# Five edits to the schedule of an attention-and-feed-forward kernel: lepe in four pieces, the reciprocal of the softmax sums on VectorE, the layer norm tiles spread, the first scores by single unit, the first rotations on VectorE alone

## The reference, cut to what matters

```python
qkv = x @ w_qkv.T + b_qkv                       # q, k, v in 16 heads of 16
q, k = elu(q) + 1, elu(k) + 1
q, k = rope(q), rope(k)                         # x1*cos - x2*sin, x1*sin + x2*cos
attn = softmax(q @ k.T / 4) @ v
lepe = depthwise conv of v along the rows, 3 taps, + b_lepe
x = layernorm(x + attn + lepe)                  # first layer norm
h = s0 * ([x, -x] @ K0); h = 2 * relu(h)        # K are matrices of +1 and -1
h = s1 * (h @ K1);       h = 2 * relu(h)
x = layernorm(x + s2 * (h @ K2))                # second layer norm
```

## Time and profile before

| | |
|---|---|
| median of 3 runs | 2399.99 us (2399.28 to 2402.57) |
| the profiled execution | 2403.18 us |
| its span, first to last instruction | 2401.3 us |
| PE busy | 2161.6 us (90%) |
| DVE busy | 1524.1 us (63%) |
| ACT busy | 1428.8 us (59%) |
| POOL busy | 1144.7 us (48%) |
| DVE reduce L908 | 1024 of 1213 ns |
| ACT exp L762 | 2048 of 607 ns |
| POOL reciprocal L1239 | 63 of 2909 ns |
| POOL lepe L1257 | 24 of 4524 ns |
| DMA, issue to landing: stacks, `k_scratch` (POOL), out, base | 2.0, 5.8, 4.1, 5.9 us |

### The profile page before, as it was taken

How to read it: one execution, slowest core, us unless ns; L and a number is a source line. 1 busy time by engine, 2 the same in 40 slices (tenths; PEclk the granted TensorE clock), 3 DMA queues, 4 the chain that set the end, 5 groups by cost and what they waited for, 6 DMA issues and landing times.

```text
span 2401.3 us, 41722 instructions
## 1 busy us (share of the span) xinstructions
PE 2161.6 (90%) x16960; PEld 839.9 (35%) x16960; DVE 1524.1 (63%) x1629; ACT 1428.8 (59%) x2601; POOL 1144.7 (48%) x726
## 2 busy tenths in 40 slices
PE   4397798999999999999989999999999999899977
PEld 2021222452225422354224622354223542244234
DVE  6766598329972499527983299725994279844432
ACT  1066597428883398625974198733986269833921
POOL 4519527662457527473276625475284733700200
PEclk8588899999999999999999999999999999899988
DMA  5001101001100101001110011001110011000000
GB/s 166 24 8 32 54 22 39 15 12 54 56 21 18 40 23 55 14 18 48 48 30 16 19 45 56 21 18 43 37 38 14 18 52 58 16 8 1 19 1 18
DMA packets 40272, 77.81 MB, mean 32 GB/s; under 512 B 15008, under 2 KB 19472, under 8 KB 36880
## 3 DMA queue, kind: packets, MB, share of 16 engines
q1 hardware_dynamic: 34896, 52.07, 7.6%
q0 software_dynamic: 5184, 23.07, 2.7%
HBM read 47.32 MB, written 25.17 MB: 30 GB/s over the span
## 4 chain that ended last, share of the span: by engine, by line
PE 55%; DVE 14%; POOL 14%; ACT 10%; issue 4%; DMA 3%; SPq 0%; ACTq 0%; POOLq 0%; DVEq 0%
PE unit_banks L670 23%; DVE maxima L908 11%; PE o_bank L592 9%; PE unit_banks L524 8%; ACT probs L762 8%; PE unit_banks L681 5%; PE unit_banks L629 4%; POOL work L1257 2%; POOL rden L1239 2%; PE unit_banks L641 2%; POOL base L1259 2%; DMA base<-in_x 1%; POOL base L1254 1%; POOL hres L1267 1%; PE unit_banks L534 1%
## 5 line engine op out<-in xcount | busy, mean ns | idle before, releaser
L908 DVE TENSOR_REDUCE maxima<-unit_banks 128x1 f32<-128x1024 f32 x1024 | 1190.3, 1213 | 134.3 <-PE unit_banks L524 129.6
L762 ACT ACTIVATE probs<-unit_banks 128x512 f32<-128x512 f32 x2048 | 1090.1, 607 | 298.7 <-PE unit_banks L534 286.5
L524 PE MATMUL unit_banks<-k_stack,q_stack 48*128 48x512 f16 x2048 | 637.0, 401 | 105.1 <-DVE maxima L908 63.4
L534 PE MATMUL unit_banks<-q_stack,k_stack 50*128 50x512 f16 x2048 | 666.2, 397 | 34.5 <-ACT probs L762 28.4
L592 PE MATMUL o_bank<-probs,v_pair 128*32 128x256 f32 x8192 | 667.3, 405 | 0.4 <-ACT probs L762 0.4
L670 PE MATMUL unit_banks<-h0T,w 128*128 128x512 f16 x2048 | 444.7, 379 | 0.0
L960 DVE SCALAR_TENSOR_TENSOR h1T<-unit_banks,h1T 128x1024 f16<-128x1024 f32 x64 | 78.4, 1224 | 414.8 <-ACT h1T L836 414.8
L1227 POOL TENSOR_TENSOR max_scaled<-maxima,ln_consts 128x16 f32<-128x16 f32 x63 | 14.6, 232 | 637.1 <-DVE maxima L908 619.9
L592 PEld LDWEIGHTS o_bank<-probs,v_pair 128*32 128x32 f32 x8192 | 171.6, 110 | 387.6 <-ACT probs L762 235.2
L524 PEld LDWEIGHTS unit_banks<-k_stack,q_stack 48*128 48x128 f16 x2048 | 117.5, 95 | 525.2 <-DVE maxima L908 279.3
L836 ACT ACTIVATE h1T<-unit_banks 128x1024 f16<-128x1024 f32 x64 | 65.5, 1023 | 388.3 <-PE unit_banks L670 388.3
(11 more groups left out here) (127 smaller groups left out, 1572.3 us busy)
## 6 DMA issues: line engine op xcount, KB each, us to landing
xT_sb<-in_xT SPq DMA_DIRECT2D x9, 1024.0 KB, 16.0
base<-in_x POOLq DMA_DIRECT2D x8, 1024.0 KB, 5.9
q_stack<-q_scratch SPq DMA_DIRECT2D x128, 64.0 KB, 2.0
k_stack<-k_scratch SPq DMA_DIRECT2D x128, 64.0 KB, 2.0
out<-hres SPq DMA_DIRECT2D x8, 1024.0 KB, 4.1
q_scratch<-parts POOLq DMA_DIRECT2D x14, 512.0 KB, 3.3
k_scratch<-parts POOLq DMA_DIRECT2D x14, 512.0 KB, 5.8
q_stack<-q_scratch SPq DMA_DIRECT2D x128, 32.0 KB, 1.9
```

Source lines behind the costliest of these rows:

```text
L524: return nc.tensor.matmul(units.half(unit[0], unit[1], half), q_stack[row:row + STACK, r, t * P:(t + 1) * P], k_stack[row:row + STACK, r, ...
L534: nc.tensor.matmul(units.half(kind, unit, 0), k_stack[row:end, r, kt * P:(kt + 1) * P], q_stack[row:end, r, half * 512:(half + 1) * 512], ...
L762: nc.scalar.activation(probs[:, 2 * (kt % 2) + h, half * 512:(half + 1) * 512], units.half(kind, unit, 0), ACT.Exp, scale=exp_regs[2 * j + ...
L908: nc.vector.reduce_max(maxima[:, parity, h * T + t:h * T + t + 1], units.both(kind, unit), AXIS_XY)\
```

## The change

Five parts. (1) `lepe` is dealt as two, two, two and one instructions behind pairs -1 to 2, and has its own temporary `lepe_tmp`, so ScalarE no longer waits for it before the projections; `ln_scales` stand right behind a piece of lepe (first layer norm) and behind `split_max` 4 (second); in batch 0 elu, rotation and split are dealt over pairs 0 to 5 with a `split_max` between every two. (2) `reciprocal_o` on VectorE in step 3 takes the place of the power on POOL. (3) `STATS_STEPS` and `NORMALISE_STEPS` are other tables. (4) In the start TensorE waits for one S unit at a time and finishes it. (5) Both first rotations are on VectorE, the high parts of the first split on ScalarE, and POOL begins lepe of batch 0 only when the first maxima are split. With these, SP loads the stack freed by pair j - 1 behind the max rows of pair j.

```diff
-STATS_STEPS = ((9, 10, 11, 12, 13, 14, 15, 16), (None, None, None, None, 35, 36, 37, 38))
-NORMALISE_STEPS = (2 * T + 6, 6 * T + 1)
+STATS_STEPS = ((7, 8, 9, 10, 11, 12, 13, 14), (None, None, None, None, 32, 33, 34, 35))
+NORMALISE_STEPS = ((17, 20, 21, 23, 25, 28, 29, 31), (37, 38, 39, 41, 44, 46, 47, 49))
...
+            def load_freed_stack(kind, b, j):
+                if j < 0:
+                    if kind != "first":
+                        units.wait_full(sp, "first" if b == 1 else "mid", b - 1, ("T", PAIRS - 1, T - 1, 0, 1))
+                        load_stacks(b, j + RING)
+                    return
+                if kind == "last" and j + RING >= PAIRS:
+                    return
+                units.wait_full(sp, kind, b, ("T", j, T - 1, 0, 1))
+                if j + RING < PAIRS:
+                    load_stacks(b, j + RING)
+                else:
+                    sp.wait_ge(scratch_written, b * 64 + 64)
+                    load_stacks(b + 1, j + RING - PAIRS)
...
-                    units.wait_full(sp, kind, b, ("T", j, T - 1, 0, 1))
-                    if j + RING < PAIRS:
-                        load_stacks(b, j + RING)
-                    else:
-                        sp.wait_ge(scratch_written, b * 64 + 64)
-                        load_stacks(b + 1, j + RING - PAIRS)
+                    load_freed_stack(kind, b, j - 1)
...
             def start_scores(v):
-                pair = [("S", -1, v, h) for h in range(2)]
                 for h in range(2):
-                    units.wait_free(pe, "start", 0, pair[h])
-                for half in range(2):
-                    for h in range(2):
-                        last = score_half(("start", pair[h]), v // T, v % T, h, half)
-                        if half == 1:
-                            last.then_inc(units.full_sem(pair[h]), 1)
+                    unit = ("S", -1, v, h)
+                    units.wait_free(pe, "start", 0, unit)
+                    for half in range(2):
+                        last = score_half(("start", unit), v // T, v % T, h, half)
+                    last.then_inc(units.full_sem(unit), 1)
...
+            for which, w in enumerate((work[:], work_of("start", 1))):
+                act.wait_ge(scale_made, SCALE_OPS[which])
+                for c, (src, dst) in enumerate(((w[:, 3], parts[:]), (w[:, 1], parts_b))):
+                    act.wait_ge(start_split, 8 * which + 3 + 3 * c)
+                    if which == 1:
+                        act.wait_ge(start_written[c], 16)
+                    nc.scalar.activation(dst[:, 0], src, ACT.Copy, scale=in_scale[:, which:which + 1]).then_inc(start_hi, 1)
...
+            def reciprocal_o(kind, b, j):
+                n = b * PAIRS + j
+                units.wait_read(dve, kind, b, ("O rows", j))
+                wait(dve, attn_written, n)
+                o = o_rows_sb[:, n % 2].rearrange("p (g c) -> p g c", c=32)
+                nc.vector.reciprocal(rden[:], o[:, :, D]).then_inc(reciprocal_done, 1)
...
+                            if h == 0 and kt == 3 and o_rows_pair(kind, j, 2) is not None:
+                                reciprocal_o(kind, b, j - 1)
...
-            rotate(combine, work_k, rotated)
+            pool.wait_ge(max_split, MAX_OPS)
...
-                    lepe(b, 0, 3)
+                    lepe(b, 0, 2)
                 split_max(kind, b, 1)
                 normalise_o(kind, b, 0)
                 if kind == "first":
                     elu(kind, b, 0)
-                    rotate_side(kind, 0)
                 else:
-                    lepe(b, 3, 6)
+                    lepe(b, 2, 4)
+                    ln_scales(b * 2 - 2, 0)
                 split_max(kind, b, 2)
                 normalise_o(kind, b, 1)
                 if kind == "first":
-                    split(kind, b + 1, 0)
-                    elu(kind, b, 1)
+                    rotate_side(kind, 0)
                 else:
-                    lepe(b, 6, 7)
-                    ln_scales(b * 2 - 2, 0)
+                    lepe(b, 4, 6)
                 split_max(kind, b, 3)
                 normalise_o(kind, b, 2)
                 if kind == "first":
-                    rotate_side(kind, 1)
-                    split(kind, b + 1, 1)
+                    split(kind, b + 1, 0)
+                else:
+                    lepe(b, 6, 7)
                 normalise_o(kind, b, 3)
+                if kind == "first":
+                    elu(kind, b, 1)
...
                 split_max(kind, b, 4)
+                if kind == "first":
+                    rotate_side(kind, 1)
+                else:
+                    ln_scales(b * 2 - 2, 1)
                 split_max(kind, b, 5)
                 normalise_o(kind, b, 4)
-                if kind != "first":
-                    ln_scales(b * 2 - 2, 1)
+                if kind == "first":
+                    split(kind, b + 1, 1)
```

61 lines of the change are left out of this document (21 added, 40 removed).

## The result

The changed kernel takes **2328.18 us** (median of 4 runs, 2321.91 to 2334.75), the kernel before 2400.51 in the same runs; the ratio is 0.9698, with a 95% interval of 0.9668 to 0.9728. It is faster by 3.0%. The profiled execution took 2330.97 us with a span of 2329.4, that is 71.9 less than the span of before, so the two traces can be laid side by side and the 71.9 dealt to places.

What follows compares the result with a forecast made beforehand. TensorE, VectorE and ScalarE bounds lie within 0.9 us per plain pair, with TensorE and ScalarE also waiting for POOL. Terms 47 + 5 + 7 - 8 + 20 + 3 = 74 from 2403.2 leave 2329, median forecast 2326, range 2304 to 2350.

Steps and rivals of the forecast that it cites:

- lepe dealt over the pairs, 47 for pairs 0 to 2: Batches 1 to 7: waits for max_parts and shift go; pairs 0 to 2 take 62.2 against 68.9, 47 us in seven.
- -8 for SyncE's order: Stack loads behind the max rows land late after the 1 MB store: 1.4 us lost in each of six batches.
- pair 0 keeps its 1.7 us wait for the max rows: Pair 0, batches 1 to 7: base's DMA, issued only 0.8 us sooner, still collides with the max rows; pair takes 20.6.
- The reciprocal: POOL loses a 2.9 us power; VectorE's added 0.25 costs nothing in plain pairs, 0.25 in pair 4, at most 16 us.
- Tiles spread, 5 and 7: Layer norm tiles spread over steps, batches 1 to 7: pair 3 gains 5 us, pairs 4 to 7 gain 7.
- Batch 0, +20: Removed max_parts waits give 32 us; a new wait of 12 for a stack load in pair 6 leaves 20.
- Start, +3: Start: VectorE's sign chain reached near 95 instead of 114.04, but held by lepe pieces, ending at 112.8: gain 3 us.
- the 49.9 of the forecast: Start: time in us counted for the rotations and first split on VectorE, with the last write at 52.32 before.
- rival A: Start: the sign chain is not held by lepe, or only in part; 2315 us, chance 0.13.
- B: Pairs 1 and 2: VectorE's and ScalarE's load replaces the waits, half of the 47 remains; 2350 us, chance 0.12.
- C: Batch 0 does not wait in pair 6, 12 us less; 2314 us, chance 0.11.
- D: Stack loads late at step 2 of every pair, slower than before; 2440 us with landing at 25.5; chance 0.04.

Runs made afterwards that it cites:

- the second run: The changed kernel run once more with nothing edited: 2326.62 us, ratio 0.9682 to the kernel before.
- the four edits: Changed kernel with SyncE's old order, base's DMA behind the first lepe product, sign instructions before first row maxima, batch 0's POOL work dealt finely: 2271.95 us.
- The experiment: Changed kernel with batch 0's elu, rotation and split on POOL dealt in small pieces between the splits of the maxima: 2310.88 us.
- the two edits: Changed kernel with VectorE's nine small sign instructions before the first row maxima and three lepe pieces before the first split of the maxima: 2320.75 us.

## Why the prediction was right or wrong

The total, 2326 against 2328.18 (2326.62 in the second run), was right, and so were most places. But pairs 0 to 2 of batches 1 to 7 came 15 short of their terms (39 forecast, 23.9 measured), and the start and pair 3 brought 19 more than theirs (8 and 27.0). That these two errors nearly cancel is luck.

*lepe dealt over the pairs, 47 for pairs 0 to 2, and -8 for SyncE's order.* Both waits of the earlier trace rows went. That the dealing does it is shown: undone alone it costs 32.9 in these pairs. Pair 2 came at 19.68 (19.6). Pair 1 without a wait for a DMA takes 21.5 to 21.7 (five batches with SyncE's order of before, all seven with the four edits), a little less than the 22.0 of the forecast. The step that failed is "pair 0 keeps its 1.7 us wait for the max rows". In before, its last step was 4.07 on average, now it is 4.99; base's DMA was issued 1.05 behind the max rows (873.21 and 874.26; in the kernel before 1.91) and the stack loads right behind, and at the start of pair 1 a second wait stands in five of seven batches, where it stood in two. The two single edits show both parts: 24 us go with base's DMA moved (7 come back behind it), 15.4 with the stack loads moved, 31.9 with both ((64.82 - 60.26) x 7). The -8 was meant for step 2 of pair 0 alone, 1.4 in each of six batches; there TensorE waited in four, 0.2 to 1.5, which measured 4.5 in all; the other 11 of SyncE's 15.4 lie in the wait for the max rows, which I had left as it was. And the 68.9 from which I counted is the way from one copy to another, the second of which had waited 1.02. From first exp to first exp, as the table cuts, the same batch takes 68.05 and the mean over seven is 68.24. That takes another 5, which the table has in pair 3. Together: pairs 0 to 2 came at 64.8 and not 62.2, 18 in seven, of which 8 were in the sum as SyncE's; with the 5 that makes the 15 between 39 and 23.9.

*The reciprocal.* In VectorE's price I was right (nothing in plain pairs: they are 18.92). In POOL's I wasn't: the 2.9 us were no part of the gain, because in pair 0 the power fitted in before VectorE would have come to its reciprocal.

*Tiles spread, 5 and 7.* Pair 3 gained 16.7. I had priced its tiles at 0.37 each from pair 6 of the earlier trace rows, as a line. They aren't one: three spread tiles cost 0.13 in the first seven steps of pair 3 (16.84 against the 16.71 of a plain pair), four 0.76 in pair 2, seven in a row 1.8 in pair 6 of the kernel before. And 1.05 a batch was carried over from the late scales, for which I had allowed 0.3. Pairs 4 to 7 gained 4.8 in this run and 8.8 in the second, around the 7; what moves is pair 4, 21.1 to 22.7 long (the 22.6 above had a mean granted clock of 0.85, with 6.8 us at 0.50), and once pair 7 (19.9 against 18.9).

*Batch 0, +20.* 18.3. The wait in pair 6 was forecast as 12 and is 11.3; the slower steps behind it (granted clock 0.50, that is 1.2 GHz, for the 9.7 us behind the wait) make it 15.7, which the forecast counted for the waits removed and not for the one added. The experiment shows that POOL's late end was the cause.

*Start, +3.* 10.3. The last write came 0.5 before the 49.9 of the forecast, and the chain was reached at 92.1 and not 95, as a tile took 2.35 and not 2.5. It took 13.9 us and not 17.8, and ended at 106.0 instead of 112.8, since three of the nine were held and not four; after that the first weight instruction, L1106, is held in their place (4.22 against 2.28). Undoing the single S units alone costs 11.1 at the start of pair 1, as much as the whole gain. The three with one element and one input, which I had counted among those that are held, took 0.15, two of them in the midst of a lepe piece. So rival A was right in part: the one-element forms with one input pass; the forms with two inputs, and of 128x3, were held wherever they began well inside a piece.

The rule of the Trainium skill on which that term leaned, "SBUF — State Buffer", section "SBUF: two separate sides" (the port pair shared with GpSimd is locked for a whole instruction), agrees for the eight small instructions that were held (one in the earlier trace rows, seven in the traces behind it), each of which ends with a lepe piece, and for the lepe piece of 6.42. For L1094 and L1095 it names no exception. "VectorE: DVE Perf Modes", section "What auto-detection actually checks", says that the mode with two ports is taken if source and destination are in SBUF and their outermost non-unit dimensions are both even or equal; whether an access of one element counts there it doesn't say, and these rows fit a no (the mode itself is in no trace).

*Rivals B, C and D.* B had just the size that came, half of the 47, but not the cause: with the waits for transfers away (the kernel with the four edits) pair 1 takes 21.7 and pair 2 19.7, so VectorE's and ScalarE's load doesn't hold the rest. C fell with 11.3 us measured, and D because no plain pair waited for its stack (18.92).

What stays open: why the waits for the max rows differ so much from batch to batch (pairs 0 to 2 took 62.8 to 67.5 with nothing different in the program). How the wait grows as base's DMA comes closer isn't shown either: with the reciprocal on POOL it was issued 1.62 behind the max rows and not 1.07, and the last step of pair 0 took 5.37 and not 4.99; only the 5.57 of the DMA moved took it away. The two transfers of the edges (127 KB each) were issued by 61.7 in the start with the two edits, and POOL began at 73.2; between 63 and 72 the DMA queues moved 23 to 25 GB/s, and why no more isn't known. The moved first rotations and the coarse order of batch 0 were not undone by themselves: what they brought is read from the traces alone.

## What to carry to other kernels

Look at what a freed microsecond sets off: here the waits of TensorE for POOL went as forecast, but pairs 0 to 2 gained 23.9 us where they gain 55.9 with no wait for a transfer left, because a 1 MB transfer and the queue of stack loads lay on four transfers of 2 KB that TensorE needs next. It pays to try a big transfer some microseconds behind the small urgent ones and not beside them; 4.6 us of other work ahead of its issue were enough here. A unit of work that "costs nothing on the idle engine" (the power on POOL) should be looked at in its place before it is moved: it may already be hidden.

## What the runs showed of the hardware that I had not expected

- VectorE beside a lepe instruction of POOL (128x2048, both inputs in SBUF): a `tensor_scalar` of 128x3 and a cast of 128x16 are held until the piece ends (4.35 each), a `tensor_scalar` of 128x1 with one input is not (0.15), a `tensor_tensor` of 128x1 is (3.96, 4.34). One `tensor_scalar` of 128x3 that began 0.01 after its piece passed (0.16). A reduce with its input in PSUM is not (1.18 each).
- It goes both ways: with VectorE's weights beside them, three lepe pieces took 6.42, 4.85 and 5.38 instead of 4.5.
- Small transfers behind or beside a 1 MB one: in batch 1 of the changed kernel the stack loads beside base landed after 3.4 to 4.0 us (medians of the four kinds), in pair 3 of the same batch after 1.9 to 2.1.
- A unit of scores made in one row group takes TensorE no longer than VectorE's reduce of 1.18, at a granted clock of 0.50: no gap in 28 units.
